# Attention by halves with heads packed on partitions, and an expert loop whose first eight tiles come from three chunks

## What is computed

```python
fl, fr = heads(h @ Wl.T), heads(h @ Wr.T)
sl, sr = leaky(fl) @ att_l, leaky(fr) @ att_r      # per head and token
p = softmax(sl[n] + sr[m], over m)
y = h + (p @ fr) @ Wf.T
x = layernorm(h + layernorm(y) * gamma + beta)
probs = softmax(x @ Wr + br); top two give the gates
y_e = relu(x @ W1[e] + b1[e]) @ W2[e] + b2[e]
out = layernorm(x + gate_1 * y_e1 + gate_2 * y_e2)
```

## Time and profile before

| | us |
|---|---|
| median of 3 runs | 225.05 |
| lowest and highest | 224.06, 227.84 |
| the profiled execution | 225.54 |
| its span, first to last instruction | 223.6 |

### The profile page before, as it was taken

The page is one execution under the profiler, slowest core; times in us unless marked ns, Lnnn a source line. Parts: engine busy times, 40 slices in busy tenths (PEclk is TensorE's granted clock), DMA queues, the critical chain, the costliest instruction groups (busy, mean ns, idle before and its releaser), DMA issues.

```text
span 223.6 us, 4699 instructions
## 1 busy us (share of the span) xinstructions
PE 151.6 (68%) x1064; PEld 131.4 (59%) x1065; DVE 137.0 (61%) x656; ACT 91.3 (41%) x227; POOL 106.6 (48%) x120
## 2 busy tenths in 40 slices
PE   0887299639481251613999999999999999980000
PEld 0345156338271241503999999999999999930000
DVE  0177988778985737421566666666666666663970
ACT  2255025231120210100565666666666666505660
POOL 2072525103778877750154445444555555532860
PEclk9999655585555555555699999999999999995555
DMA  6999995000111111112122222222222222119131
GB/s 163 375 430 426 425 352 74 0 3 1 49 48 36 46 52 51 60 48 48 24 63 72 70 71 70 71 71 71 71 70 61 71 70 69 40 38 311 63 141 47
DMA packets 18187, 24.16 MB, mean 108 GB/s; under 512 B 2624, under 2 KB 15232, under 8 KB 17152
## 3 DMA queue, kind: packets, MB, share of 16 engines
q1 hardware_dynamic: 15216, 18.03, 25.2%
q0 software_dynamic: 2528, 5.22, 7.3%
q10 hardware_dynamic: 432, 0.80, 1.1%
HBM read 16.71 MB, written 7.32 MB: 107 GB/s over the span
## 4 chain that ended last, share of the span: by engine, by line
PE 51%; POOL 15%; issue 11%; DVE 10%; DMA 7%; SPq 2%; ACT 1%; ACTq 0%; POOLq 0%; DVEq 0%
PE bank L997 20%; PE bank L1009 19%; POOL x_rows L508 12%; PE bank L990 3%; DMA ht_sb<-h_t 2%; DVE bst L614 2%; PE bank L871 2%; DMA ht_sb<-y_rows 2%; PE bank L874 2%; POOL rstd L473 2%; DVE ht_sb L836 1%; PE bank L921 1%; PE bank L882 1%; DMA x_rows<-x_rows,slot 1%; DVE mv L617 1%
## 5 line engine op out<-in xcount | busy, mean ns | idle before, releaser
L520 POOL DMA_INDIRECT y_rows<-yo,dst x47 | 45.0, 957 | 54.4 <-DVE yo L769 54.1
L997 PE MATMUL bank<-xt,leaky_r 128*128 128x128 f32 x376 | 51.5, 282 | 0.0
L1009 PE MATMUL bank<-w_sb,leaky_l 128*128 x376 | 50.1, 277 | 0.0
L997 PEld LDWEIGHTS bank<-xt,leaky_r 128*128 128x128 f32 x376 | 47.4, 198 | 0.0
L1009 PEld LDWEIGHTS bank<-w_sb,leaky_l 128*128 128x128 f32 x376 | 46.4, 195 | 0.0
L420 ACT ACTIVATE leaky_l<-bank,by_q 128x128 f32<-128x128 f32 x94 | 29.4, 363 | 40.4 <-PE bank L997 40.4
L508 POOL DMA_INDIRECT x_rows<-x_rows,slot x32 | 31.2, 976 | 9.3 <-issue 9.3
L412 ACT ACTIVATE leaky_r<-w_sb 128x512 f32 x47 | 29.7, 631 | 12.5 <-DVE bank L733 8.0
L762 DVE TENSOR_SCALAR leaky_l<-bank,by_q 128x128 f32<-128x128 f32 x94 | 30.3, 347 | 3.5 <-PE bank L997 1.1
L769 DVE COPY yo<-bank 128x128 f32<-128x128 f32 x47 | 13.7, 291 | 27.9 <-PE bank L1009 27.9
L756 DVE COPY xt<-bank 128x128 f32<-128x128 f32 x47 | 13.3, 284 | 8.8 <-PE bank L990 7.3
(11 more groups left out here) (138 smaller groups left out, 235.8 us busy)
## 6 DMA issues: line engine op xcount, KB each, us to landing
w_sb<-w SPq DMA_DIRECT2D x8, 1024.0 KB, 15.9
xg<-x_rows SPq DMA_DIRECT2D x47, 65.0 KB, 1.8
x_rows<-pad_rows SPq DMA_DIRECT2D x1, 1040.0 KB, 24.1
ht_sb<-h_t SPq DMA_DIRECT2D x4, 256.0 KB, 7.2
h_sb<-h SPq DMA_DIRECT2D x4, 256.0 KB, 7.6
h_sb<-y_rows SPq DMA_DIRECT2D x4, 256.0 KB, 4.5
ht_sb<-y_rows SPq DMA_DIRECT2D x4, 256.0 KB, 4.7
out<-h_beta SPq DMA_DIRECT2D x4, 256.0 KB, 2.1
```

Source lines behind the costliest of these rows:

```text
L520: nc.gpsimd.indirect_dma_start(y_rows[:, :], bass.IndirectOffsetOnAxis(ap=dst[:, q:q + 1], axis=0), yo[:, q % DEPTH, :], None).then_inc(sc ...
L997: ins = nc.tensor.matmul(ps_h[k % 2][half][:, (c % 2) * P:(c % 2 + 1) * P], w1_now[:, k % 2, c * P:(c + 1) * P], xt[:, k % 2, :], start=Tr ...
L1009: ins = nc.tensor.matmul(ps_y[k % 2][:, 0:D], hid[:, k % 2, c, :], w2_sb[:, bass.ds(e * F + c * P, P)], start=c == 0, stop=c == FC - 1)
```

## The change

- Attention runs on two halves of four sequences each (`NHALF`, `HW` = 1024 tokens). The score vectors are spread over 32 columns, and the four sequences of a half go to partitions 0, 32, 64 and 96 of one 128x256 tile, so Exp, maximum and sum run once on 256 columns for a half. The sum over tokens is a matmul with h stationary (`pool_h`), then `apart` and `cross` give a 128x512 `mixer`; each chunk of four tiles is then one 128x512 matmul (`mix`).
- No power on POOL: ACT takes Sqrt of the variance (`dev1`, `dev2`), DVE its reciprocal and the shift (`scaling`). ACT does all four tiles of both normalisations. gamma and beta are two 128x512 steps of DVE.
- After three chunks the full tiles are counted (at most eight, `QE`), and the tables for the first eight tiles are made (`count`, `offsets`, `rows`, `tables` with r = 0); SP may fetch these once 24 scatters are done. The tables for the other 39 tiles follow after chunk 3. PE and DVE begin the loop behind both (`by_q_ready` 2). POOL issues chunk 3's eight scatters ahead of the y scatters.
- The loop uses one pair of banks for the up-projections and one bank for x; `up` waits for the relus of the tile before. b2, now held as 1 MB in SBUF, is added by DVE as y is copied out. Rows beyond a tile's end are given an index out of bounds and not written. ACT makes a diagonal 128x128 of each gate in 32 of the tiles.
- The tail adds x1 and both gated y by matmuls in PSUM, in five groups of 4, 4, 4, 2 and 2 tiles; DVE takes the statistics from there, ACT normalises from there.
- Loads: h_t's first two chunks go first on SP's queue, first_params on ACT's, the pad rows ahead of the weights. h, h_t, y and the output are laid out anew, so that a partition reads 2 KB in one piece.

```diff
-STAGES = (("project", 0), ("scores", 5.82), ("factors", 5.92), ("weigh", 8.96), ("scales", 10.96),
...
-STARTS = (0, 6.12, 14.12, 22.12)
...
+HALF_STAGES = (("right", 0), ("left", 1.5), ("scores_r", 2.5), ("scores_l", 4.0), ("turn_col", 5.0), ("pool_h", 6.0),
+CHUNK_STAGES = (("mix", 0), ("moments1", 1), ("dev1", 2.5), ("norm1", 3.0), ("affine", 5.0), ("moments2", 6.5),
+HALF_STARTS = (0, 7.0)
+CHUNK_STARTS = (9.0, 18.0, 28.0, 38.0)
+TABLE_STAGES = (("count", 0), ("offsets", 1.5), ("rows", 2.5), ("tables", 4.0))
+TABLE_STARTS = (("early", 28.0 + 18.5), ("last", 38.0 + 18.5))
...
+            def fetch(q, k, i, part):
+                if known(q) and q == 0:
+                    sp.wait_ge(tiles_ready, 1)
+                    sp.wait_ge(dispatched[0], 16 * K2 * TC * (NCH - 1))
...
+            for q in range(QE):
+                fetch(q, q % DEPTH, q // DEPTH, 0)
+            sp.wait_ge(tiles_ready, 2)
+            sp.wait_ge(dispatched[1], 16 * K2 * TC)
+            with sp.Fori(QE // DEPTH, Q // DEPTH) as i:
+                for k in range(DEPTH):
+                    fetch(DEPTH * i + k, k, i, 0)
+            for q in range(DEPTH * (Q // DEPTH), Q):
+                fetch(q, q % DEPTH, Q // DEPTH, 0)
...
+            def scores_r(s):
+                act.wait_ge(negmax_ready, s + 1)
+                nc.scalar.activation(col[:, s, :], ps_sr[:, 0:N], ACT.Exp, bias=negmax[:, s:s + 1],
+                                     accum_out=tot[:, s:s + 1]).then_inc(col_ready, 1)
+
+            def scores_l(s):
+                act.wait_ge(drop_ready, s + 1)
+                nc.scalar.activation(row[:, s, :], drop[:, s, :], ACT.Exp, scale=-1.0)
+                nc.scalar.activation(rrow[:, s, :], drop[:, s, :], ACT.Exp).then_inc(row_ready, 1)
...
+                act.wait_ge(g_ready, s + 1)
+                for b in range(HB):
+                    rows = slice(LANES * b, LANES * (b + 1))
+                    ins = nc.scalar.activation(mixer[rows, s, b * D:(b + 1) * D], ps_sr[rows, 0:D], ACT.Copy)
+                ins.then_inc(mixer_ready, 1)
+
+            def deviation(n, j):
+                act.wait_ge(mv_ready[n], j + 1)
+                nc.scalar.activation(dev[:, n, j, :], mv[:, n, j, :, 1], ACT.Sqrt,
+                                     bias=views["eps"]).then_inc(dev_ready[n], 1)
...
+            def norm1(j):
+                act.wait_ge(shift_ready[0], j + 1)
+                for t in range(TC):
+                    ins = nc.scalar.activation(z_sb[:, j % 2, t, :], y_sb[:, j % 2, t, :], ACT.Identity,
+                                               scale=rstd[:, 0, j, t:t + 1], bias=shift[:, 0, j, t:t + 1])
+                ins.then_inc(z1_ready, 1)
...
-            def rank(j):
-                act.wait_ge(exin_ready, j + 1)
-                nc.scalar.activation(exo[:, tiles(j), :], exin[:, tiles(j), :], ACT.Exp).then_inc(exo_ready, 1)
...
+            act.wait_ge(exin_ready, 1)
+            nc.scalar.activation(exo[:, :, :], exin[:, :, :], ACT.Exp).then_inc(exo_ready, 1)
...
             def relu_high(q, k):
-
                 act.wait_ge(up_high, q + 1)
-                if not known(q) or q >= 2:
-                    act.wait_ge(down_done, q - 1)
                 for c in range(FC // 2, FC):
-                    ins = nc.scalar.activation(hid[:, k % 2, c, :],
-                                               ps_h[k % 2][1][:, (c % 2) * P:(c % 2 + 1) * P], ACT.Relu,
+                    ins = nc.scalar.activation(hid[:, k % 2, c, :], ps_h[1][:, (c % 2) * P:(c % 2 + 1) * P], ACT.Relu,
                                                bias=by_q[:, c, bass.ds(q, 1)])
                 ins.then_inc(relu_act, 1)
...
+                if part == 1:
+                    nc.scalar.activation(diag[:, bass.ds(q - DIAG_FROM, 1), :].rearrange("p o d -> p (o d)"),
+                                         views["ident"], ACT.Copy, scale=g12[:, bass.ds(q - DIAG_FROM, 1)])
+
+            loop(act, step, (DIAG_FROM // DEPTH, (DIAG_FROM + NT * K2) // DEPTH))
+
+            nc.scalar.activation(std[:, NT:NT + 1], views["eps"], ACT.Sqrt).then_inc(diag_ready, 1)
...
-            def rsqrt(n, j):
-
-                pool.wait_ge(mv_ready[n], j + 1)
-                if n == 0:
-                    nc.gpsimd.tensor_tensor(rstd[:, n, j, :], ve[:, n, j, :], views["minus_half"],
-                                            ALU.pow).then_inc(rstd_ready[n], 1)
-                    return
-                link(nc.gpsimd.tensor_tensor(rstd[:, n, j, :], ve[:, n, j, :], views["minus_half"], ALU.pow))
-                nc.gpsimd.tensor_tensor(shift[:, n, j, :], negmean[:, n, j, :], rstd[:, n, j, :],
-                                        ALU.mult).then_inc(rstd_ready[n], 1)
...
+            def dispatch(j):
+                pool.wait_ge(slot_ready, j + 1)
+                pool.wait_ge(x1_ready, j + 1)
...
+                                             yo[:, q % DEPTH, :], None, bounds_check=YROWS - 1,
+                                             oob_is_err=False).then_inc(scattered[q % DEPTH], 16)
...
+            def scores_l(s):
+
+                dve.wait_ge(sl_ready, s + 1)
+                if s == 0:
+                    dve.wait_ge(negmax_ready, 1)
+                link(nc.vector.tensor_scalar(peak[:, s, :], ps_sl[:, 0:N], negmax[:, s:s + 1], None, ALU.subtract))
+                nc.vector.scalar_tensor_tensor(drop[:, s, :], peak[:, s, :], negmax[:, s:s + 1], ps_sl[:, 0:N], ALU.add,
+                                               ALU.subtract).then_inc(drop_ready, 1)
...
+            def scaling(n, j):
+                dve.wait_ge(dev_ready[n], j + 1)
+                link(nc.vector.reciprocal(rstd[:, n, j, :], dev[:, n, j, :]))
+                nc.vector.scalar_tensor_tensor(shift[:, n, j, :], mv[:, n, j, :, 0], -1.0, rstd[:, n, j, :], ALU.mult,
+                                               ALU.mult).then_inc(shift_ready[n], 1)
...
+                link(nc.vector.tensor_tensor(z_sb[:, j % 2, :, :], z_sb[:, j % 2, :, :],
+                                             views["gamma"].unsqueeze(1).to_broadcast([P, TC, D]), ALU.mult))
                 dve.wait_ge(hbeta_ready, j + 1)
...
+                link(nc.vector.tensor_tensor(y_sb[:, j % 2, :, :], z_sb[:, j % 2, :, :], h_beta[:, tiles(j), :],
+                                             ALU.add))
...
-            def copy_y(q, k, i):
+            def add_b2(q, k, i):
+
+                dve.reg_load(held[k % 2], bank[0:1, bass.ds(q, 1)])
+                e = dve.snap(held[k % 2], min_val=0, max_val=E - 1)
                 dve.wait_ge(down_done, q + 1)
                 if not known(q) or q >= DEPTH:
                     dve.wait_ge(scattered[k], 16 * i)
-                nc.vector.tensor_copy(yo[:, k, :], ps_y[k % 2][:, 0:D]).then_inc(yo_ready, 1)
-
-
-
-            def index_parts(q, k, n=2):
...
+            def scores_r(s):
+                if s:
+                    pe.wait_ge(mixer_ready, s)
+                pe.wait_ge(leaky_r_ready, 2 * s + 2)
+                for b in range(HB):
+                    ins = nc.tensor.matmul(ps_sr[LANES * b:LANES * (b + 1), 0:N], views["att_r"],
+                                           leaky_r[:, s, b * N:(b + 1) * N], start=True, stop=True,
+                                           tile_position=(0, LANES * b))
+                ins.then_inc(sr_ready, 1)
...
+                for b in range(HB):
+                    for u in range(2):
+                        ins = nc.tensor.matmul(ps_small[:, 256 + H * b:256 + H * (b + 1)],
+                                               h_sb[:, 2 * TC * s + TC * u + b, :], col_tok[:, s, u, b, :],
+                                               start=u == 0, stop=u == 1)
+                ins.then_inc(z_ready, 1)
...
+                nc.tensor.matmul(ps_sr[:, 0:D], heads[:, s, :, :].rearrange("d b k -> d (b k)"), views["wf_t"],
+                                 start=True, stop=True).then_inc(g_ready, 1)
...
+                nc.tensor.matmul(ps_chunk[j][:, :], scale[:, s, u * P:(u + 1) * P], mixer[:, s, :], start=True,
+                                 stop=True).then_inc(fh_ready, 1)
...
-                nc.tensor.transpose(ps_x[k % 2][:, 0:P], xg[:, k % DEPTH, 0:D], ident).then_inc(xt_done, 1)
+                if not known(q) or q:
+                    pe.wait_ge(xt_copied, q)
+                nc.tensor.transpose(ps_x[:, 0:P], xg[:, k % DEPTH, 0:D], ident).then_inc(xt_done, 1)
...
                 for c in range(FC):
                     half = c // 2
-                    ins = nc.tensor.matmul(ps_h[k % 2][half][:, (c % 2) * P:(c % 2 + 1) * P],
+                    if not known(q) or q:
+                        if c == 0:
+                            pe.wait_ge(relu_dve, 2 * q)
+                        if c == FC // 2:
+                            pe.wait_ge(relu_act, q)
+                    ins = nc.tensor.matmul(ps_h[half][:, (c % 2) * P:(c % 2 + 1) * P],
```

(24 more changed lines are left out.)

1084 lines of the change are left out of this document (540 added, 544 removed).

## The result

The changed kernel takes 227.44 us, the median of four runs (227.02 to 230.87), against 224.56 us of the kernel before beside it: a ratio of 1.0134, 95% interval 1.0092 to 1.0177. That is inside 2%, and inside the range of 216 to 231, but 3 us slower where I had forecast half a microsecond faster. Some executions of one and the same kernel are slow ones (230.87 of these four, and three of the four of experiment 10, the profiled one among them), and ratios and intervals leave them out. The profiled execution took 227.02 for a span of 225.2.

The account below looks back on a forecast made before the run. It took POOL's scatters to set the end of the front and TensorE to be never idle in the loop. Front -0.2, loop 0, tail -0.3 gave -0.5 us: span 223.1, time 224.5, range 216 to 231.

Parts of the forecast that it names:

- S0: Point in the front where chunk 0's last normalisation may start; forecast at 43.35 us.
- Removing the bound of GpSimd's scatters: Front: 24 scatters, not 32, ahead of fetches for eight tiles; freedom all spent on a slower chain, -0.2 us.
- The first half at full clock: Attention's first half: pooling of h done at 17.2 us, second half's right projections at 18.9, mixer ready at 25.2.
- The score steps: Attention in the front: four 32x256 score matmuls on four column groups take 1.1 us at full clock, 2.1 at half.
- rival A: Score matmuls in the front: column groups run at once, 0.86 us at half clock; time 222.0; chance 0.19.
- Four chunks: Front, from chunk 0's last normalisation to chunk 3's: steps of 11.9, 14.35 and 14.6 us, 40.85 together.
- Last tables: End of the front: tables ready 18.65 us after chunk 3's normalisation may start, first up-projection 1.8 later, at 104.65.
- The loop: Expert loop: still 1.90 us a tile; new relu waits have 0.3 us in hand each, so costed at nothing.
- Rival C: Expert loop: single banks make TensorE wait for relus, 0.15 us a tile, 6.9 in all; time 231.4; chance 0.22.
- The tail: After the loop: 0.35 us late at half clock, 0.95 early if the clock rises during the sums; middle taken, -0.3.
- B: Front: TensorE's clock stays full or comes back, saving 4.8 us, then another 8 to 9; priced at 217; chance 0.31.
- D: Front alone slower: score matmuls in a row, 3.4 us not 2.1, twice, plus 1 us; 228.1; chance 0.06.

Follow-up runs that it names:

- experiment 10: The kernel of experiment 8 with unread matmuls on TensorE ahead of each chunk's transposes only; median 212.56 us of four runs, lowest 207.62, kernel before 225.45.
- Experiment 6: The changed kernel with SP's first fetch behind all 32 scatters, not 24, so that the early tables serve nothing; 234.10 us, ratio 1.0232.
- Experiment 3: The changed kernel with nine unread 128x512 projections in TensorE's idle stretches of the first 38 us; 223.38 us, ratio 0.9896.
- experiment 1: The changed kernel with GpSimd's four h + beta steps issued together, ahead of the first scatters; 223.32 us, ratio 0.9916.
- the second comparison: The changed kernel run once more as it is, beside the kernel before; 228.96 us against 229.85, ratio 0.9963.
- experiment 8: The changed kernel with beta steps ahead of scatters, TensorE kept busy in the first 38 us, earlier loop banks, chunks 9.0 apart; 216.16 us, ratio 0.9415.
- experiment 9: The kernel of experiment 8 with unread projections on TensorE also in its waits of the chunk stages and tables; 223.28 us, ratio 0.9675.
- the kernel before, again: The kernel before the change, run once more as it is to get a second profile; 229.79 us.
- experiment 7: The kernel of experiment 1 with the four chunks starting 9.0 apart in the table, not 9, 10 and 10; 224.04 us, ratio 0.9702.

## Why the prediction was wrong

The sum missed by 2.1 us of span: +4.2 in the front, +1.0 in the loop, nothing in the tail and -3.2 in the close. The front's 4.2 are 3.4 us up to S0 (the first half, priced at a full clock that it didn't have), 1.2 in the four chunks (3.35 for the h + beta steps, priced at nothing, less 2.1 by which the rest of my count was too large) and -0.4 in the last tables.

**Removing the bound of GpSimd's scatters.** Right: the scatters no longer set the start of the loop; the chain of chunks and last tables does. Experiment 6 gives the early tables' worth, 7.5 us. "24 scatters' worth of freedom" is misread, though: only chunk 3's eight no longer stand ahead of the loop.

**The first half at full clock** failed: "eight matmuls with h stationary (at full clock half of 0.43 each) 17.2, the second half's right projections 18.9". They ended at 20.9 and 24.5. In the prediction TensorE's only idle stretch that mattered was the 2.4 us ahead of mix, and the clock fell there. It fell some 10 us earlier, at 15, behind the wait for GpSimd's leaky part, which I had timed from 10.6 to 13.3 without looking at TensorE meanwhile. The mixer was ready at 30.5 instead of 25.2. Then the clock was full for the mix, where I had it fallen: I was wrong once in each direction. Experiment 3 puts the price of the slow clock in this part at 2.9 to 3.8 us.

**The score steps**: rival A's mechanism was right, 0.64 and 1.06 in place of 1.1 and 2.1. Mix and both scores of the second half took 2.6 us where I had 6.0. That gave back part of the 5.3 us by which the mixer was late: S0 came 3.4 late.

**Four chunks** was right in kind (which blocks DVE waits for, the order, the short first step), with 42.1 against 40.85. Taking out the 3.3 us of experiment 1 leaves 38.7, so the rest of my count was 2.1 us too large and hid most of the error: 0.8 in the first step, and in the others the argmax block (1.95 where I read 2.25) and the handovers that I had added. The step that failed is one that isn't there: h + beta was given no place in GpSimd's queue, where it stands behind scatters, and no claim on DVE. In chunk 2 DVE had to wait for its result, in chunk 3 DVE was held while it ran.

**Last tables**: 20.1 us from chunk 3's normalisation to the first up-projection, forecast 20.45.

**The loop** at nothing failed by 1.04. "So the new waits have 0.46 and 0.44 us in hand, less a handover of 0.15: 0.3 each" is read from one tile between two turns. Once behind the gates the second relu ended late and up had to wait for it; at the later turns the waits cost time though the relus had ended, and how is open. Rival C had the place right and the price, 6.9, six times too high.

**The tail**: -0.3 was right in the sum, not in its parts. The clock did rise during the sums, as in the better of my two cases, which gave 0.95. But y landed 7.9 us behind the loop's end, where the earlier trace rows have 6.1 and the prediction "as before"; SP issued the first read 0.6 later, and it took 1.2 longer to land. From there on the tail was 2.0 us shorter than before (13.2 instead of 15.2), 1.1 more than that case gave. That the two nearly cancel is luck.

```profile
209.37 1.84 PE L1072 MATMUL bank<-h_sb,diag 128*128 128x128 f32 x8 [4.30 <-DMA h_sb<-y_rows]
```

**The close** I took over from before, 5.84 us, without asking what it was. It was GpSimd's, 3.2 us of it, and in the changed kernel GpSimd's last step stands 12.6 us sooner. With a row for it the sum would have been further off, -3.7: by luck this error hid 3.2 of the others' 5.3.

**Rivals.** B, at 0.31, stands refuted as stated: the clock did not stay. Experiments 3 and 10 measure what it priced: 2.9 to 3.8 in the first part and 5.1 in the chunks and tables, 8 to 9 together, near the 7.5 that I had taken; B's parts, 4.8 and 8 to 9, were too large. D is refuted by the rows of the scores. The second rule of the Trainium skill (a drain of 1.38 us besides the table load, "ScalarE: Activation LUTs", section "What ACT_TABLE_LOAD costs") has no trace here either: from the end of one row of ACT at 36.32 to the start of the next at 37.63, whose data had been ready since 34.7, it is 1.31 us with the load of 1.28.

## What to carry to other kernels

Ask of every section what ends it, the close too: here a step on GpSimd near the end cost 6.6 us of drain behind it. A step that is given to GpSimd is a claim on two queues, its own behind whatever stands there and, as two DVE steps with both inputs in SBUF showed, DVE's while it runs. Where TensorE does little, walk through its idle stretches one by one before pricing its work, and test keeping it busy: here that in the first 38 us, beta and the chunks reordered and the loop's banks given back took the changed kernel from 1.3% over the kernel before (or level with it, by the second comparison) to 5.9% under it in experiment 8, and keeping TensorE busy in the chunks brought 5 us more.

## What the runs showed that I had not expected

- GpSimd's closing DRAIN ends 6.6 us behind the end of its last step in three kernels, whether that step is a product of 0.20 us, a copy of 0.19 or a scatter of 0.98.
- DVE steps of 0.69 and 0.16 us, both with two inputs in SBUF, took 2.35 and 1.84 beside a GpSimd addition of 1.27; one of 0.68 with an input in PSUM took no longer beside another.
- The clock fell with TensorE busy (at 32.2 us in the changed kernel, 18.6 in experiment 3), 1.6 and 1.5 us behind the end of idle stretches of 2.26 and 0.98 us.
- Matmuls whose rows end at 66.7 (experiment 9), 84.25 (the kernel before, again) and 76.70 (experiment 7) were followed by their waiters only at 77.1, 89.4 and 80.3. The rows' ends are modelled, so such a row doesn't tell when the waiter may go; whether the matmul or the signal behind it was late isn't shown.
